# A rank-64 diagonal mask, a new order of the attention stage, and two steps moved in a transformer layer on one Trainium2 core

## The reference

```python
logits = einsum('bihd,bjhd->bhij', q, k) * scale + SLOPES * (pos_j - pos_i)
logits = where(i >= j, logits, -inf)
out = einsum('bhij,bjhd->bihd', softmax(logits), v).reshape(B, T, D) @ Wout
x = layernorm(x + out)
gate, up = x @ wg.T, x @ wu.T
x = layernorm(x + (silu(gate) * up) @ wd.T)
```

## Time and profile before

| | |
|---|---|
| median of three runs | 2225.71 us (2225.01 to 2226.89) |
| the profiled execution | 2225.28 us, of it the span from first to last instruction 2223.6 us |
| mean granted TensorE clock | 0.974 of 2.4 GHz |
| PE busy / weight loads | 2029.4 us (91%) / 1562.9 us (70%) |
| VectorE / ScalarE / GpSimd busy | 1604.0 us (72%) / 1259.5 us (57%) / 933.5 us (42%) |
| mean time of one exponential, L708 | 1024 ns (640 of them) |
| mean time of one row maximum, L784 to L786 | 1212 to 1221 ns (640 of them) |

### The profile page before, as it was taken

One profiled execution on the slowest core, in us unless ns is written; L12 is line 12 of the kernel. 1 busy time (PEld: TensorE's weight loads), 2 busy tenths in 40 slices (PEclk: granted clock), 3 DMA queues, 4 the chain that ended last, 5 costly groups with the idle time before them and its releaser, 6 DMA issues.

```text
span 2223.6 us, 47880 instructions
## 1 busy us (share of the span) xinstructions
PE 2029.4 (91%) x19236; PEld 1562.9 (70%) x19236; DVE 1604.0 (72%) x2766; ACT 1259.5 (57%) x1999; POOL 933.5 (42%) x1924
## 2 busy tenths in 40 slices
PE   4779999999999999999999999999999999999986
PEld 3447677677677677767767767767767767777766
DVE  4557777777777777777777777777777777777754
ACT  1436655556655555655655665655665555565552
POOL 0123444444444443444443444444444444344444
PEclk7889999999999999999999999999999999999998
DMA  8355354355444445445445535435545545544400
GB/s 212 84 116 106 95 121 91 96 118 120 91 112 102 93 109 120 102 101 110 98 97 121 112 96 116 96 90 122 114 97 113 102 93 110 120 100 94 92 20 20
DMA packets 148830, 229.15 MB, mean 103 GB/s; under 512 B 13552, under 2 KB 64496, under 8 KB 148592
## 3 DMA queue, kind: packets, MB, share of 16 engines
q1 hardware_dynamic: 148608, 226.09, 46.1%
HBM read 140.05 MB, written 84.93 MB: 101 GB/s over the span
## 4 chain that ended last, share of the span: by engine, by line
PE 62%; DVE 17%; ACT 7%; POOL 6%; issue 4%; DMA 2%; SPq 1%; POOLq 0%; ACTq 0%; DVEq 0%
PE pair L476 57%; PE pair L479 5%; ACT probs L708 4%; DVE row_max L786 4%; DVE row_max L781 3%; POOL h_lo L893 3%; DVE h_full L842 2%; DVE attn_lo L769 2%; DVE row_max L784 2%; POOL x L906 2%; DVE h_full L838 1%; DMA q_rows<-max_lo 1%; DVE stats L826 1%; POOL rstd L903 1%; DVE x L822 1%
## 5 line engine op out<-in xcount | busy, mean ns | idle before, releaser
L708 ACT ACTIVATE probs<-pair 128x1024 f32<-128x1024 f32 x640 | 643.0, 1024 | 464.2 <-PE pair L476 456.8
L886 POOL TENSOR_SCALAR_AFFINE_SELECT probs<-probs 128x256 f32<-128x256 f32 (+1 forms) x896 | 374.6, 443 | 464.3 <-ACT probs L708 457.0
L893 POOL TENSOR_TENSOR h_lo<-h_full,h_hi 128x256 fp32r<-128x256 f32 x384 | 283.5, 739 | 593.3 <-ACT h_hi L733 589.4
L786 DVE TENSOR_REDUCE row_max<-pair 128x8 f32<-128x1024 f32 x256 | 312.7, 1221 | 101.7 <-PE pair L476 101.6
L476 PE MATMUL pair<-k_rows,q_rows 52*128 52x512 f32 (+3 forms) x2048 | 318.8, 369 | 64.0 <-DVE row_max L786 21.1
L476 PE MATMUL pair<-probs,v_ones 128*32 128x512 f32 (+3 forms) x4096 | 340.8, 451 | 24.5 <-ACT probs L708 21.8
L476 PEld LDWEIGHTS pair<-k_rows,q_rows 52*128 52x128 f32 x2048 | 172.2, 189 | 266.0 <-DVE row_max L786 94.9
L784 DVE TENSOR_REDUCE row_max<-pair 128x2 f32<-128x1024 f32 x256 | 310.2, 1212 | 35.5 <-PE pair L476 35.5
L476 PE MATMUL pair<-q_rows,k_rows 64*128 64x512 f32 (+3 forms) x2048 | 313.8, 364 | 12.3 <-DMA q_rows<-max_lo 10.3
L725 ACT ACTIVATE h_full<-pair 128x256 f32<-128x256 f32 x384 | 146.7, 382 | 149.5 <-PE pair L476 148.7
L476 PE MATMUL pair<-mask_half,ident_half 64*128 64x256 bf16 (+1 forms) x2560 | 231.1, 259 | 0.0
(11 more groups left out here) (89 smaller groups left out, 3505.8 us busy)
## 6 DMA issues: line engine op xcount, KB each, us to landing
bounce<-staged_hi SPq DMA_DIRECT2D x128, 256.0 KB
bounce<-staged_lo SPq DMA_DIRECT2D x128, 256.0 KB
q_rows<-bounce SPq DMA_DIRECT2D x128, 256.0 KB, 5.0
k_rows<-bounce SPq DMA_DIRECT2D x128, 256.0 KB, 6.4
x_sb<-L_attn_x SPq DMA_DIRECT2D x32, 512.0 KB, 10.5
k_rows<-bounce SPq DMA_DIRECT2D x128, 128.0 KB, 5.6
q_rows<-bounce SPq DMA_DIRECT2D x128, 128.0 KB, 7.0
x<-L_attn_x SPq DMA_DIRECT2D x32, 512.0 KB, 9.0
```

The source lines that it names most:

```text
L708: scalar.activation(probs[g][:, tile, :, :], pair[:, :, :], ACT.Exp, scale=scale).then_inc(s_exp, 1)
L786: vector.tensor_reduce(maxima[:, QB2_PARTS:QB0 + 1, :, p].rearrange("p b s -> p s b"), pair[:, :, :].rearrange("p s (b n) -> p s b n", n=P ...
L886: made = pool.affine_select(out=diagonal, in_=diagonal, compare_op=ALU.is_ge, fill=0.0, base=0, pattern=[[0, diagonal.shape[1]], [1, P]], ...
L893: pool.tensor_tensor(h_lo[:, m, :], h_full[(n_split_h[step] - 1) % H_BUFFERS][:, :], h_hi[:, m, :].bitcast(F32), ALU.subtract).then_inc(s_ ...
```

## The change

Five edits. (1) The first pass's mask is made of columns: each masked block of 128 keys is cut into two halves of 64 columns, and each half gets one product of depth 64 per head. The "stair" (moving, 64 columns) is the same for both halves, its last row is all masked, and `turned` (weights) says which query takes which row of it. The count of matmuls stays at 4 for a tile, their columns become 64 in tiles 0 and 2 and 128 in the others. (2) The stage's order is a table, `ATTENTION`: scores come ahead of the first pass, and the parts of the weighted sums stand behind F2, S4, F7 and S9 in place of S1, S2, S7 and S8. (3) Between the two parts the pair that holds the weighted sum isn't given to scores: they take the older of the pairs not held. (4) `project(w+2, 1)`, the keys, with its spread, is the last step of the rest, behind `down` and the norms; in even windows `max_row` comes one feed-forward tile earlier and the queries one group of tiles later. (5) In odd windows `norm1(done, 0)` goes from ahead of the sixth h_lo to behind `norm2`.

```diff
-PV_AFTER = {1: (-2, 1, 0), 2: (-2, 1, 1), 7: (-1, 0, 0), 8: (-1, 0, 1)}
+ATTENTION = ((S, 0), (F, 0), (S, 1), (F, 1), (S, 2), (F, 2), (V, -2, 1, 0), (S, 3), (F, 3), (F, 4), (S, 4), (V, -2, 1, 1),
+             (S, 5), (F, 5), (S, 6), (F, 6), (S, 7), (F, 7), (V, -1, 0, 0), (S, 8), (F, 8), (F, 9), (S, 9), (V, -1, 0, 1))
...
+    stair = np.where(np.arange(HALF)[None, :] > np.arange(HALF)[:, None], np.float32(MASKED), np.float32(0)).astype(np.float32)
+    stair[HALF - 1] = MASKED
+    turned = np.zeros((2, HALF, P), np.float32)
+    turned[0, :, :HALF] = turned[1, :, :HALF] = turned[1, :, HALF:] = np.eye(HALF)
+    turned[:, HALF - 1, :] = 0
+    turned[1, HALF - 1, :HALF] = 1
...
-                pair = score_pairs[scores_made % 2]
-                scores_made += 1
+            elif what == S and self.has(w - 1):
+                pair = next(p for p in self.by_age(score_pairs) if p != held)
...
             if has_ffn:
-                self.gate_up(ffn, 0, range(0, 3))
+                self.gate_up(ffn, 0, range(0, 2))
             self.max_row(w)
+            if has_ffn:
+                self.gate_up(ffn, 0, range(2, 6))
             self.project(w + 2, 0)
             if has_ffn:
-                self.gate_up(ffn, 0, range(3, 6))
+                self.down(ffn, 0)
             self.project(w + 2, 1)
-            if has_ffn:
-                self.down(ffn, 0)
...
             self.project(w + 2, 0)
-            self.project(w + 2, 1)
...
             if has_done:
-                self.add("norm1", done, 0)
                 self.project_out(done, 2)
             if has_ffn:
                 self.down(ffn, 1)
             if has_done:
+                self.add("norm1", done, 0)
                 self.add("norm1", done, 2)
+            self.project(w + 2, 1)
...
+                    n = len(range(*masked.indices(blocks)))
+                    for c in range(2):
+                        made = both(lambda s: halves[:, s, masked, c, :], lambda r: turned[r:r + HALF, c, :],
+                                    lambda r: stair[r:r + HALF, 0:n, :], False, c == 1)
```

More of the change, by code:

```diff
@@ L65, in constants @@
     identity = np.eye(P, dtype=np.float32)
-    mask = np.where(np.arange(P)[None, :] > np.arange(P)[:, None], np.float32(MASKED), np.float32(0)).astype(np.float32)
-    halves = [np.concatenate([table[a * HALF:(a + 1) * HALF]] * 2) for table in (identity, mask) for a in range(2)]
-    return rows, np.stack([identity] + halves, 1)
+    stair = np.where(np.arange(HALF)[None, :] > np.arange(HALF)[:, None], np.float32(MASKED), np.float32(0)).astype(np.float32)
[4 more added lines that the diff above has]
+    turned[1, HALF - 1, :HALF] = 1
+    planes = [turned[0], turned[1], np.concatenate([stair, stair], 1)]
+    return rows, np.stack([identity] + [np.concatenate([table, table]) for table in planes], 1)
 class Plan:
@@ L102, in take, with by_age @@
         self.occupy(step, [min(range(BANKS), key=lambda i: self.used[i])])
+    def by_age(self, pairs):
+        return sorted(pairs, key=lambda i: max(self.used[2 * i:2 * i + 2]))
     def has(self, u):
@@ L107, in attention @@
     def attention(self, w):
-        pairs = sorted(range(BANKS // 2), key=lambda i: max(self.used[2 * i:2 * i + 2]))
+        pairs = self.by_age(range(BANKS // 2))
         score_pairs, first_pairs = [pairs[1], pairs[3]], [pairs[0], pairs[2]]
-        scores_made = 0
-        for k in range(2 * TILES):
-            if self.has(w):
+        held = None
+        for what, k, *rest in ATTENTION:
+            if what == F and self.has(w):
                 pair = first_pairs[k % 2]
@@ L122, in attention @@
                 self.add("select", w - 1, k)
-            offset, g, part = PV_AFTER.get(k, (0, 0, 0))
-            u = w + offset
-            if offset and self.has(u):
+            elif what == V and self.has(w + k):
+                u, (g, part) = w + k, rest
                 if part == 0:
-                    self.occupy(("pv", u, g, 0), [2 * score_pairs[scores_made % 2]])
-                    scores_made += 1
+                    held = self.by_age(score_pairs)[0]
+                    self.occupy(("pv", u, g, 0), [2 * held])
                 else:
@@ L540, in rows @@
                         return lambda r: buffer[r:r + PASS1_ROWS, p, c0:c0 + n]
+                    halves = pair[:, :, :].rearrange("p s (b c n) -> p s b c n", b=blocks, c=2)
                     if tile == 4:
+                        masked = slice(1, 4, 2)
                         for a in range(2):
@@ L545, in _ @@
                             both(lambda s: pair[:, s, a * 256:(a + 1) * 256], rows(q, p, P, P), rows(k, p, 0, 256), a == 0, False)
-                        for a in range(2):
-                            made = both(lambda s: pair[:, s, :].rearrange("p (b n) -> p b n", n=256)[:, :, P:256],
-                                        lambda r: ident_half[r:r + HALF, a, :], lambda r: mask_half[r:r + HALF, a, :, :], False, a == 1)
                     elif tile % 2 == 0:
+                        masked = slice(3, 4)
                         p = 2 * g + tile // 2
                         both(lambda s: pair[:, s, :], rows(q, p, 3 * P, P), rows(k, p, 0, 4 * P), True, False)
-                        for a in range(2):
-                            made = both(lambda s: pair[:, s, 3 * P:4 * P],
-                                        lambda r: ident_half[r:r + HALF, a, :], lambda r: mask_half[r:r + HALF, a, 0, :], False, a == 1)
                     else:
+                        masked = slice(2, 4)
                         p = 2 * g + tile // 2
@@ L558, in _ @@
                         both(lambda s: pair[:, s, 3 * P:4 * P], rows(q, p, 0, P), rows(k, p, 0, P), False, False)
-                        for a in range(2):
-                            made = both(lambda s: pair[:, s, 2 * P:4 * P].rearrange("p (b n) -> p b n", n=P),
-                                        lambda r: ident_half[r:r + HALF, a, :], lambda r: mask_half[r:r + HALF, a, :, :], False, a == 1)
+                    n = len(range(*masked.indices(blocks)))
+                    for c in range(2):
+                        made = both(lambda s: halves[:, s, masked, c, :], lambda r: turned[r:r + HALF, c, :],
+                                    lambda r: stair[r:r + HALF, 0:n, :], False, c == 1)
                     made.then_inc(s_first, 1)
```

15 lines of the change are left out of this document (7 added, 8 removed).

## The result

The changed kernel takes **2171.57 us** (median of four runs, 2170.71 to 2172.58); the kernel before, run beside it, 2226.24 us. The ratio is 0.9755, with a 95% interval from 0.9738 to 0.9772. The profiled execution has a span of 2170.9 us against 2223.6 before. The forecast was 2176 us, between 2142 and 2205.

What follows compares the result with a forecast made beforehand. The prediction took TensorE's work (busy 1830 of 1940 us) and its waits, clock included, as the bound. It summed 2225.3 - 50 + 11 - 11 = 2175.3 us, said 2176, and gave a range of 2142 to 2205.

Steps and rivals of the forecast that it cites:

- Term 1: Odd rests: with norm1 moved, `down` no longer waits 1.61 us for the last h_lo; 31 rests, 50 us less.
- Term 4: Moved key projection and its spread: put at 0, as was the start-up, with bounds of -6 and +4 us.
- Term 2: Attention stage, new order and mask: -0.17 us behind even rests, +0.54 behind odd ones; +11 us, bounds -11 and +34.
- Term 3: Clock drops behind the odd rest's wait: taken as gone with that wait, 11 x 1.09 = -11 us, bounds -12 and 0.
- Rival (a): Clock behind odd rests: the drops stay, giving 2187 us; chance 0.10.
- Rival (b): Head of all 64 stages: the clock falls at every one, 1.09 us each, giving 2246 us; chance 0.08.
- rival d: Odd rests: the spread lands late and ScalarE stands still at staged_hi; 31 us at 1 us beyond cover, 2207; chance 0.06.
- Rival (c): Attention stage: gets shorter than laid out, half a microsecond a stage, giving 2144 us; chance 0.14.
- (e): First-pass mask: 64 columns cost what 128 did, giving 2176 to 2182 us; chance counted within the forecast's 0.57.

Runs made afterwards that it cites:

- norms late: Both norm1 steps moved into the next even window's stage, ahead of its sixth score tile, against the changed kernel: 2146.14 us, ratio 0.9647.

## Why the prediction was right, point by point

**Term 1 (-50 us) held in size, but not alone.** The wait is gone and the odd rest, from the last group of one stage to the first of the next, is shorter by 18.51 - 16.77 = 1.74 us with 1.61 forecast. Moved alone, though, the norm gained nothing (65.67 a pair). The forecast had the reason in its numbers without saying so: it started residual2 1.28 us *ahead* of the stage, which is so only because the key projection is last. That head start is what left V0' 0.67 us of wait instead of the 1.3 and 1.7 measured without it. I booked the moved projection at 0 in term 4 and its effect in term 2, where no reader would look for it. Between the change and the change with keys back lie 99 us.

**Term 2 (+11 us) held nearly to the row.** The waits forecast at S4 and S9 are there; at S7 none was long enough to be listed. Against the layout from S0's start (1151.81): S1 1.48 (forecast 1.47), F2 2.62 (2.60), V0 3.13 (3.11), S4 5.74 (5.69), V1 6.17 (6.12), V0' 10.26 (10.20), V1' 13.31 (13.22), the end 14.74 (14.66). Behind an odd rest V0' 10.99 (10.91) and the end 15.48 (15.37). The trace shows the wait of S1 as 0.67 and not 0.83 us, since 0.15 of it passes as longer busy time of the group ahead. "What the mask saves falls nearly all ahead of a wait" held in this order: 0.14 us a pair. A pair got 1.22 us shorter, with 1.24 forecast.

**Term 3 (-11 us) had the right size by luck, and the wrong cause.** The drops went, and they were worth 11.3 us. But "with the wait gone I take them as gone" fails: with the wait put back (41.8 us of it) none returned, and keys last alone removed all ten with the wait in full. What differs is what follows the wait: 0.67 us of `down` and then the head of the stage with its own waits, or 2.07 us of `down` and projection. That the dense stretch is the reason is my reading; the runs show only that moving it there ended the drops. Nor is the rest of the condition known: before the change the same wait stood behind 29 odd rests, and ten of them, mostly every third, had a drop. Rival (a), drops that stay, did not come about. The rule of the Trainium skill ("TensorE: Matmul & The Clock Gate", "Why this matters for your kernels"), by which a gap this short should do no harm, was weighed in the prediction; the runs bear neither it nor my forecast out as they stand. Gaps of 1.45 and 1.7 us can go with a drop in this kernel, and the same gap of 1.44 us with a dense stretch behind it did not. Rival (b), a clock that falls at every stage behind the 0.83 us, was wrong: not one of 57 such waits was followed by a drop.

**Term 4 (0) was mis-sized: the start-up gave 10 us**, outside its bounds of -6 and +4. Waits for transfers up to the sixth stage, first of the kernel before, then of the changed one:

```profile
PE pair L476 <- DMA q_rows<-bounce: 18.5, 4, 9.2
...
PE pair L476 <- DMA q_rows<-max_lo: 9.9, 4, 3.7
```

```profile
PE pair L486 <- DMA q_rows<-max_lo: 16.0, 4, 7.8
...
PE pair L486 <- DMA q_rows<-bounce: 2.3, 1, 2.3
```

28.4 us became 18.3. In the start-up the rests are short, the stage catches up with its gather and with `store_max`, and any microsecond of SyncE's queue is on the path. Every kernel with keys last starts its sixth stage at 182 to 190 us, every one without at 191.6 to 197.3. Keys last alone gave 5.0 us; how the other five divide among the order, the mask and the clock, which is at the lower level for 61 us there before the change and for 55 after it, these runs don't settle. The regular part had the cover that the forecast names: no wait for `staged_hi` came (rival d).

**The end of the run was not in the sum.** It is 4.0 us longer. The last stage has no first-pass tiles, so it comes to V0' sooner (9.23 us in, where a regular stage behind an odd rest gets there at 10.32). And no key projection is left ahead of it to cover the moved norms, so the select that it needs comes later (12.37 against 10.99 us in):

```profile
2093.45 1.94 PE L486 MATMUL pair<-probs,v_ones 128*32 128x512 f32 x8 [3.14 <-POOL probs L894]
```

```profile
2092.70:2102.94 10.24, 8.36 (x51) 4.49 (x52) 0.48 (x1) 3.50 (x5) 3.45 (x9) 0.50 0.01 2
```

TensorE stands 3.14 us, and the clock is at half for the next 10.24. With the norms late this part took 3.8 us less.

So the total was hit by right sizes in the regular part (-50 + 11 - 11 = -50 us against -46.7) and by two small parts of opposite sign at its ends, -10.0 and +4.0, of which the first was put at 0 and the second was not seen. That these two came to -6 us, close to the 3.3 by which the regular part fell short, is luck. Rival (c), a stage half a microsecond shorter, did not come about, nor did (e): 64 columns stand 0.07 us ahead of the next score tile in the old order, 128 stand 0.10.

## What to carry to other kernels

Ask of a step that fills a gap not only what it costs where it stands, but whom it gives time: six matmuls moved behind `down`, with no work saved, were worth nothing in the pair of the kernel before and yet carried both the norm's move and the clock. Moving work off one wait pays only as far as the engine that takes it over has slack before its next reader; lay out that engine to the first instruction that waits for it (here GpSimd to V0'), and put the work behind the urgent items of its queue, not ahead of them. And price a part of a bundle in the bundle's own order: the mask is worth 0.14 us a pair in the new order of the stage and 0.62 to 0.71 in the old one.

## What the runs showed of the hardware

- In these traces the length of a wait alone does not tell whether the clock falls. A wait of 1.44 us with 2.07 us of dense matmuls behind it left the clock at 2.4 GHz in all 29 odd rests; the same wait with the stage right behind it was followed by ten drops in 29, and one of 1.7 us inside a stage with a 0.91 us wait earlier by 24 in 29. Waits of 0.67 us were followed by none in the new order and by four in the old one, where V0' stands behind three more waits of 0.2 to 0.3 us. Which of several equal waits gets the drop, no run here shows.
- A drop within the regular part lasted 3.4 or 6.8 us and cost 0.33 to 0.36 us for each us of it, not a half. Part of the reason is that waits are taken up: with the keys back TensorE is busy for all 6.80 us of the drop shown, and S9, which waits 0.29 us for its exponential in a stage without a drop, doesn't wait there. Whether that is all of the difference isn't shown.
- A group of four bf16 mask matmuls of depth 64 moved the next matmul by 0.10 us with 128 columns and by 0.15 with 256, whatever the mask holds; both were far less than the durations shown for the groups (0.29 and 0.40 us).
